# A top-k attention kernel: third comparison taken as a difference on GpSimd, one list of neighbours in place of two, image tokens embedded three batches at a time

## The reference

```python
tok = patches @ W + b                       # 36 patches of 768 values
h = layernorm(concat([cls, tok]) + pos) * gamma + beta
h = concat([h, txt])                        # 165 x 256
q, k, v = heads(layernorm(h) @ W_qkv.T + b_qkv)      # 16 heads of 16
scores = q @ k.T * scale                    # 16 x 165 x 165
topk_scores, indices = top_k(scores, 49)    # int(165 * 0.3)
attn = softmax(scores where in the top 49, else -inf)
h = h + (attn @ v) @ W_out.T + b_out
h = h + ffn(layernorm(h))                   # shared FFN, and 64 routed experts, 128 slots each
```

## Time and profile before

| | us |
|---|---|
| median of three runs | 3370.57 |
| profiled execution | 3362.61 |
| its span, first to last instruction | 3360.9 |
| PE busy | 2740.0 (82%) |
| DVE busy | 2809.3 (84%) |
| ACT busy | 2785.1 (83%) |
| POOL busy | 2167.3 (64%) |

### The profile page before, as it was taken

How to read it: one execution, slowest core, us unless ns; L and a number is a source line. 1 busy time by engine, 2 the same in 40 slices (tenths; PEclk the granted TensorE clock), 3 DMA queues, 4 the chain that set the end, 5 groups by cost and what they waited for, 6 DMA issues and landing times.

```text
span 3360.9 us, 82985 instructions
## 1 busy us (share of the span) xinstructions
PE 2740.0 (82%) x22281; PEld 2098.7 (62%) x22281; DVE 2809.3 (84%) x11013; ACT 2785.1 (83%) x12673; POOL 2167.3 (64%) x3409
## 2 busy tenths in 40 slices
PE   4688888888888888888888888988888888647776
PEld 3466666666666666666666666666666666436665
DVE  1899999999999999999999999999999999822222
ACT  3999999999999999999999999999999999611111
POOL 3456767667676667767766676776676766444554
PEclk7899999999999998999999999999999999868888
DMA  1001100000000000000000000000000000016776
GB/s 51 11 14 20 20 21 21 21 21 20 14 20 20 21 21 21 21 15 19 20 20 21 21 21 21 18 17 20 20 21 21 21 20 17 11 38 158 174 176 139
DMA packets 181453, 116.34 MB, mean 35 GB/s; under 512 B 100208, under 2 KB 172484, under 8 KB 180964
## 3 DMA queue, kind: packets, MB, share of 16 engines
q1 hardware_dynamic: 146596, 91.60, 10.0%
q0 software_dynamic: 34368, 19.34, 3.9%
HBM read 66.51 MB, written 33.40 MB: 30 GB/s over the span
## 4 chain that ended last, share of the span: by engine, by line
DVE 38%; ACT 27%; PE 13%; issue 12%; DMA 4%; POOL 3%; DVEq 1%; SPq 1%; POOLq 0%; ACTq 0%
ACT JK L831 14%; DVE PR L1175 6%; DVE S L1028 5%; DVE ML L1070 5%; DVE MU L1047 4%; ACT E L819 4%; DVE XU L1037 4%; ACT SIDE L850 4%; DMA E<-x_rows,ids_t 2%; DMA out<-E,ids_t 2%; PE bank L1521 2%; DVE XL L1057 2%; PE bank L1676 1%; DVE RD L1180 1%; ACT PTT L861 1%
## 5 line engine op out<-in xcount | busy, mean ns | idle before, releaser
L831 ACT ACTIVATE JK<-S,thr 128x165 f32<-128x165 f32 x2688 | 1124.0, 442 | 3.4 <-POOL thr L562 1.7
L607 POOL DMA_INDIRECT slot_token<-TOKI,SLOT x512 | 541.3, 1057 | 202.8 <-issue 182.6
L850 ACT ACTIVATE SIDE<-S,t 128x165 f32<-128x165 f32 x1344 | 572.4, 447 | 9.4 <-POOL t L574 4.4
L831 ACT ACTIVATION_READ_ACCUMULATOR JK<-S,thr 128x1 f32 x2688 | 565.0, 210 | 0.0
L819 ACT ACTIVATE E<-bank,nb 128x165 f32<-128x165 f32 x1344 | 523.8, 418 | 14.6 <-DVE S L1028 14.4
L1175 DVE SCALAR_TENSOR_TENSOR PR<-S,TV,E 128x165 f32<-128x165 f32 x1344 | 434.1, 379 | 0.0
L1028 DVE TENSOR_SCALAR_CACHE_REDUCE S<-bank 128x165 f32<-128x165 f32 x1344 | 357.9, 314 | 12.5 <-PE bank L1504 10.5
L1047 DVE MAX8 MU<-XU 128x8 f32<-128x165 f32 x1344 | 349.2, 311 | 0.2 <-DVE XU L1037 0.2
L1070 DVE MAX8 ML<-XL 128x8 f32<-128x165 f32 x1344 | 339.7, 307 | 0.7 <-POOL XL L589 0.7
L1037 DVE SCALAR_TENSOR_TENSOR XU<-SIDE,S 128x495 f32<-128x495 f32 x448 | 317.0, 708 | 11.9 <-ACT SIDE L850 11.4
L589 POOL TENSOR_TENSOR XL<-SIDE,S 128x495 f32<-128x495 f32 x256 | 308.0, 1203 | 28.9 <-ACT SIDE L850 14.3
(11 more groups left out here) (196 smaller groups left out, 6981.8 us busy)
## 6 DMA issues: line engine op xcount, KB each, us to landing
S<-in_w_gate SPq DMA_DIRECT2D x64, 192.0 KB, 2.7
S<-in_w_up SPq DMA_DIRECT2D x64, 192.0 KB, 3.3
S<-in_w_down SPq DMA_DIRECT2D x64, 192.0 KB, 3.4
x_rows<-X SPq DMA_DIRECT2D x64, 160.0 KB
H<-in_txt SPq DMA_DIRECT2D x64, 128.0 KB, 5.9
QA<-QT SPq DMA_DIRECT2D x512, 10.3 KB
QB<-QT SPq DMA_DIRECT2D x512, 10.3 KB
out<-OT SPq DMA_DIRECT2D x64, 128.0 KB
```

Source lines behind the costliest of these rows:

```text
L607: pool.indirect_dma_start(slot_token, bass.IndirectOffsetOnAxis(SLOT[r % 2][:, 0, k:k + 1], 0), TOKI[r % 2][:, :], None, bounds_check=SLOT ...
L831: act.activation(JK[:, t % 4, :], S[r % 2][:, t, :], ACT.Sign, bias=(t0, t1)[n][:, t:t + 1], scale=-1.0, accum_out=(c0, c1)[n][:, t:t + 1] ...
L850: act.activation(SIDE[:, t % GROUP + GROUP * (g % 2), :], S[r % 2][:, t, :], ACT.Sign, bias=t2[r % 2][:, t:t + 1], scale=-1.0, accum_out=c ...
```

## The change

**Third count and lists.** POOL subtracts the third threshold from `S` and scales by 2^-40, tile by tile, into one of five buffers `X` (`apart`); `under`, `above` and `side` are gone, and so are `SIDE`, `XU` and `XL`. The count is taken from the sign of `X`: on ACT for groups 0 to 2 (into `JL`, 9 tiles), on DVE for groups 3 to 6 (into `JD`, 12 tiles). From the count DVE works out for each row on which side of `t2` the 49th entry lies (`side`, `side2`, `sides`) and writes a word `flip`; an exclusive or of `flip` with the bits of `X` (`one_side`) turns the tile so that one MAX8 (`nearest`) gives the eight entries on that side. `rank`, `candidates` and `threshold` then work on one list of eight for the wanted entry and its neighbour together.

```diff
-            def under(i, r, g):                      # POOL, groups 0, 2, 4, 6
-                pool.wait_ge(s_cnt, CN * i + 2 * NT + GROUP * (g + 1))
...
-                pool.tensor_tensor(XL[g % 3][:, :, :], SIDE[...], S[...], ALU.mult).then_inc(s_xp, 1)
+            def apart(i, r, g):                      # POOL, all seven groups
+                n = NG * i + g
+                pool.wait_ge(s_up, UP * i + (17 if g < AHEAD // GROUP else 20))
+                if n >= DEEP:
+                    pool.wait_ge(s_list, GROUP * (n - DEEP + 1))
+                for t in range(GROUP * g, GROUP * (g + 1)):
+                    last = pool.tensor_scalar(X[n % DEEP][:, t % GROUP, :], S[r % 2][:, t, :], t2[r % 2][:, t:t + 1], DOWN,
+                                              ALU.subtract, ALU.mult)
+                last.then_inc(s_xp, 1)
...
-            def side(i, r, g):                       # ACT, 21 tiles: Sign of S against t2 into SIDE, sum into c2
+            def third_count(i, g):                   # ACT, groups 0 to 2
...
+                    act.activation(JL[:, n % 3, :], X[(NG * i + g) % DEEP][:, k, :], ACT.Sign, bias=tiny[:, :], scale=-1.0,
+                                   accum_out=c2[:, t:t + 1]).then_inc(s_c2, 1)
+            def third_count(i, g):                   # DVE, groups 3 to 6
...
+                    dve.tensor_scalar(JD[:, n % 3, :], X[(NG * i + g) % DEEP][:, k, :], 0.0, None, ALU.is_lt, ALU.add,
+                                      accum_out=c2[:, t:t + 1]).then_inc(s_cd, 1)
+            def one_side(i, g):
...
+                at = flip[:, GROUP * g:GROUP * g + GROUP].rearrange("p (n a) -> p n a", a=1).to_broadcast([P, GROUP, T])
+                bits = X[n % DEEP][:, :, :].bitcast(i32)
+                dve.tensor_tensor(bits, bits, at.bitcast(i32), ALU.bitwise_xor).then_inc(s_x, 1)
-                    dve.max(MU[:, t, :], XU[g % 2][:, t % GROUP, :]).then_inc(s_mu, 1)
-                    dve.max(ML[:, t, :], XL[g % 3][:, t % GROUP, :]).then_inc(s_ml, 1)
+                    dve.max(LIST[:, 0, WIN * t:WIN * t + WIN], X[n % DEEP][:, t % GROUP, :]).then_inc(s_list, 1)
```

```diff
+            def load_image(b, r):
+                n, at = (b + PACKED - 1) // PACKED, IMG * ((b + PACKED - 1) % PACKED)
+                ahead(sp, s_bd, BD * (b - RING) + 3, b - RING)
...
+                sp.dma_start(H[r][0:IMG, 1, :], HP[at:at + IMG, :]).then_inc(s_txt[r], 16)
...
-                    last = pe.matmul(bF[0:IMG, 0:D], PT[r % 2][:, k, :], WT[:, k, :], start=(k == 0), stop=(k == PK - 1))
+                    last = pe.matmul(bF[0:TRIO, 0:D], PT[:, k, :], WT[:, k, :], start=(k == 0), stop=(k == PK - 1))
```

More of the change, by code:

```diff
@@ L60 @@
 LOW = -3.0e38
-BIG = 3.0e38
 GONE = -1.0e38
@@ L131, in early_fusion_kernel @@
         JK = sb("JK", [P, 4, T])
-        SIDE = sb("SIDE", [P, 2 * GROUP, T])
+        JL = sb("JL", [P, 3, T])
+        JD = sb("JD", [P, GROUP, T])
+        W = [JD[:, k, :] for k in range(GROUP)]
         sz = sb("sz", [P, NT])
@@ L289, in parcels, with share, trio, of_trio @@
             return 16 * sum(m > 0 or at == PACKED - 1 for m in range(n % 2, n + 1, 2))
+        def share(i, groups, g):
+            return len(groups) * i + sum(k < g for k in groups)
+        TRIOS = (n_batch + PACKED - 1) // PACKED
+        def trio(m):
+            return m % PACKED == 0 and 0 <= m // PACKED < TRIOS
+        def of_trio(n):
+            return [b for b in range(PACKED * n - PACKED + 1, PACKED * n + 1) if b >= 0]
         def known(i):
@@ L645, in iteration @@
                 if has(i - 1):
-                    under(i - 1, (r - 1) % RING, 0)
-                if has(i + 1):
-                    front_scale(i + 1)
+                    apart(i - 1, (r - 1) % RING, 4)
+                if trio(i + 4):
+                    front_scale((i + 4) // PACKED)
+                if has(i):
+                    guess(i, r, 0)
+                if has(i - 1):
+                    apart(i - 1, (r - 1) % RING, 5)
+                    apart(i - 1, (r - 1) % RING, 6)
+                if has(i - 4):
+                    back_slots(i - 4, r, 0, 2)
@@ new lines, in span, with side @@
+            def span(k):
+                return GROUP * SETS[k][0], GROUP * SETS[k][-1] + GROUP
+            def side(i, k):
+                lo, hi = span(k)
+                if SETS[k][0] in THIRD:
+                    dve.wait_ge(s_cd, GROUP * share(i, THIRD, SETS[k][-1] + 1))
+                    scale, base = -8.0, -4.0 * (MIDDLE - T)
+                else:
+                    dve.wait_ge(s_c2, GROUP * share(i, BY_ACT, SETS[k][-1] + 1))
+                    scale, base = -4.0, -4.0 * MIDDLE
+                if k == 0:
+                    ahead(dve, s_turn, TN * i, i - 1)
+                gated()
+                dve.tensor_scalar(off[:, lo:hi], c2[:, lo:hi], scale, base, ALU.mult, ALU.add).then_inc(s_turn, 1)
@@ L1342, in iteration @@
                 if has(i - 1):
-                    uppers(i - 1, 3)
+                    side2(i - 1, 1)
+                if has(i):
+                    take(i, r, 5)
+                if has(i - 1):
+                    third_count(i - 1, 6)
+                    one_side(i - 1, 3)
                 if has(i - 3):
@@ L1355, in iteration @@
                 if has(i - 1):
[L1356 removed]
+                    one_side(i - 1, 6)
+                    places(i - 1)
+                    nearest(i - 1, 4)
+                    places2(i - 1)
                 if has(i - 3):
                     back_weights2(i - 3, (r - 3) % RING)
+                if has(i - 1):
+                    nearest(i - 1, 5)
+                    rank(i - 1)
+                    nearest(i - 1, 6)
+                if has(i - 3):
                     back_place(i - 3)
                 if has(i - 1):
[L1361 removed]
+                    candidates(i - 1)
                 if has(i - 3):
                     back_place2(i - 3)
+                if has(i - 1):
+                    threshold(i - 1)
+                if has(i - 3):
                     back_place3(i - 3)
                 if has(i - 1):
[L1366 removed]
+                    threshold2(i - 1)
                 if has(i - 3):
@@ L1653, in iteration @@
                     sure(i - 1)
+                if trio(i + 5) and i > -1:
+                    front_embed((i + 5) // PACKED)
                 if has(i + 1):
```

721 lines of the change are left out of this document (363 added, 358 removed).

## The result

The changed kernel takes 3651.18 us (median of 4 runs, 3645.12 to 3651.91), beside 3371.27 us for the kernel before on the same chip. The ratio is 1.0837, with a 95% interval of 1.0798 to 1.0877: slower by 8%, where I forecast 3200 us, 5% faster. The profiled execution has a span of 3650.2 us.

What follows compares the result with a forecast made beforehand. POOL was to bound at 41.6 us per batch, DVE just behind; with 0.4 of waits 42.0, so 2.7 x 64 = 173 us less, 3 more at the start, 8 for the median: 3200 us, range 3090 to 3340.

Steps and rivals of the forecast that it cites:

- the price of the 21 differences on POOL: POOL's added threshold subtractions, priced like `KZ` at 407 ns plus a 0.08 gap: 10.2 us per batch, plus 1.0.
- The bounds: POOL's period with every difference at 402 ns, 40.5 us; at the mean 509, 42.8; at 758, 48.
- POOL becomes the fullest engine: After the change POOL, at 41.6 us per batch, was to bound the kernel, with DVE a microsecond behind.
- the lock decides: Rival: POOL and DVE block each other at shared SBUF ports, 758 ns per difference, 3620 us; chance 0.06.
- DVE, busy: DVE per batch: 44.7 less 14.6 removed plus 10.55 added, 40.6 us, branch and waiting included.
- the branch 1.65: DVE's "issue" wait at the head of each iteration, for the branch of `general`: 1.65 us per batch, unchanged.
- POOL, taken: POOL's time per batch, busy plus gaps and "issue" time: 37.6 - 5.0 - 2.2 + 10.2 + 1.0 = 41.6 us.
- meeting DVE: Allowance on POOL for differences disturbed by running beside DVE: 1.0 us per batch.
- the "issue" ahead of the transfers: Time ahead of POOL's indirect transfers in which it waits for nobody, counted as taken: 4.5 us per batch.
- The trio: Embedding three batches as one, saving per batch 2.2 us on POOL, 0.8 on DVE and 1.8 on PE.
- Late image rows: Rival: the image rows' transfer lands after 9 us, `front_norm` waits 2.6 us; period 43.3, 3285 us; chance 0.08.
- The waits added: DVE waiting 1 to 1.5 us for POOL, ACT before its last nine tiles' first count; 0.4 us per batch counted.

Runs made afterwards that it cites:

- m1: Test without the reference's work: POOL runs seven instruction forms, 24 each, alone and beside DVE; add and multiply 0.38 us, subtract and multiply 0.83.
- e1_add: The changed kernel with the 21 differences written as addition of the negated threshold; 3160.48 us, ratio to the kernel before 0.9406.
- e2: The kernel before with only the embedding changed, three batches embedded as one; 3374.15 us, ratio 1.0051.
- e8: The kernel before with three batches embedded as one and POOL's `XL` waiting for the `XU` of its group; 3436.00 us, ratio 1.0145.

## Why the prediction was wrong

**The step that failed** is the price of the 21 differences on POOL. The prediction put it as "`KZ` is the same instruction: 128x165, one operand per partition, two operations, SBUF to SBUF", so 21 x 0.487 + 1.0 = 11.2 us. `KZ` is the same opcode with the same shape, but it adds and multiplies; the difference subtracts and multiplies. I compared everything that the row shows, and the row does not show the operation. It stood in the code, two lines to compare. Measured: a step of 0.83 alone (m1), a mean of 929 ns in the kernel, and 19.1 us for 21 where the sum had 11.2. With the operation turned into an addition the median is 404 ns and the step 0.39, 8.2 us for 21.

**The bounds failed with it.** All three, 402, 509 and 758 ns, were rows of that one instruction. They bounded how much it can be disturbed, not what another operation costs. The rows of POOL with other operations, `XL` and the affine, were in the table and not used: the affine's two steps take 721 and 1619 ns for 256 elements, which for 165 would be 0.46 and 1.04 us.

**The mechanism was right only at the wrong price.** "POOL becomes the fullest engine" holds in the changed kernel: it is busy or in its own gaps for about 47.9 of 49.1 us. At the price that I had assumed it does not hold, as the table below shows: in e1_add DVE and ACT are the fullest again.

**The rival "the lock decides"** had 3620 us, 0.9% below what was measured, for the wrong reason. It wanted each difference at 758 ns by contention and "decides from a mean step of 0.63 us". The step did pass 0.63, but 20 of the 21 are slow where DVE is not in the way. Contention is in it with one difference per batch, at 2.99 us in place of 0.85. I gave 0.06 to a time that had two ways to come about, of which I saw one. The Trainium skill ("SBUF — State Buffer", "Who interferes with whom") is borne out in its direction by m1: MAX8, with one input, costs POOL nothing and products with two inputs do. A block, and not a sharing, fits the difference of 2.99 us and DVE's product of 29.07; the 0.26 us that each quick difference of m1 loses is less than a whole product (0.43).

**The other terms**, checked on e1_add, which has the price that I assumed:

| term, us per batch | predicted | e1_add |
|---|---|---|
| period | 42.0 | 41.5 |
| DVE, busy | 40.6 less the branch 1.65 and waits 1.1 = 37.9 | 37.9, with 3.6 idle |
| ACT | 37.4 | 37.8 |
| PE | 36.6 | 859 / 1000 x 41.5 = 35.7 |
| POOL, taken | 41.6 | 30.6 busy, 10.9 idle, of which 5.1 waiting: 36.4 |

The sums on DVE, ACT and PE hold within 1 us. POOL's did not even then: of its idle time 3.3 us stand ahead of indirect transfers and 5.1 are waits for ACT and DVE, so it is taken for some 36 us, not 41.6. Of the 5.2 us too many, 3.0 are the differences (8.2 against 11.2: the 1.0 for meeting DVE and most of the gap of 0.08 were not there) and 1.2 the "issue" ahead of the transfers (3.3 against 4.5). In e1 DVE is idle for 1.5 us per batch at the head of its iteration, where the branch stands, and for 0.7 ahead of the fourth group's scores; ACT's largest wait, 2.4 us for the first copy of scores, stands at the same head. The rest of DVE's 3.6 us is spread over small waits, and no run shows which chain sets the 41.5. That 42.0 came out so near is luck: it was POOL's sum, 5 us too high, and DVE's own stood just beside it.

**The trio.** The prediction took 2.2 us from POOL and 0.8 from DVE as gains; in the old order they gave nothing (e2), because POOL then collided with DVE (`XU` 712 to 821 ns there, 661 in e8). **Late image rows** did not occur: in e1 the wait for `HP`'s transfer totals 2.7 us in four cases. **The waits added** stood ahead of DVE's first count as named, at two to three times the size, since POOL was late; ACT's stood ahead of its first twelve tiles and not its last nine.
